# Order of the weighted expert sums in the last stage of a two-layer state-space and mixture-of-experts kernel

## What is computed

```
x = x + tanh(g_xattn[0]) * L0_xattn(ctx, layernorm(x))   # state-space scan, 16 states
x = x + tanh(g_ffn[0])   * L0_ffn(layernorm(x))          # 16 experts, 4 per token, and a shared one
x = x + tanh(g_xattn[1]) * L1_xattn(ctx, layernorm(x))   # a second scan
x = x + tanh(g_ffn[1])   * L1_ffn(layernorm(x))          # dense product, 8 low-rank experts, 2 per token
...
out, _ = jax.lax.scan(body, jnp.zeros_like(x), (gate_proj, up_proj, down_proj, cw.T))   # sum over experts of cw * y
```

## Time and profile before

| | us |
|---|---|
| median of 3 runs | 1586.72 |
| the runs | 1582.42, 1586.72, 1589.91 |
| profiled execution, own time | 1583.32 |
| its span | 1581.6 |
| DVE busy over the span | 1413.3 (89%) |
| TensorE busy, as modelled | 1255.5 (79%) |
| POOL busy | 794.9 (50%) |
| ScalarE busy | 836.6 (53%) |

### The profile page before, as it was taken

The page is one execution under the profiler, slowest core; times in us unless marked ns, Lnnn a source line. Parts: engine busy times, 40 slices in busy tenths (PEclk is TensorE's granted clock), DMA queues, the critical chain, the costliest instruction groups (busy, mean ns, idle before and its releaser), DMA issues.

```text
span 1581.6 us, 13941 instructions
## 1 busy us (share of the span) xinstructions
PE 1255.5 (79%) x4244; PEld 697.7 (44%) x4244; DVE 1413.3 (89%) x1462; ACT 836.6 (53%) x1341; POOL 794.9 (50%) x413
## 2 busy tenths in 40 slices
PE   6785677898689768977869998899988888806768
PEld 2321232443244224443526666566665666504444
DVE  4899989989999999998997999999899999967774
ACT  5754837473675455434855665556654444414332
POOL 0465446535553553360464556655556665575522
PEclk9898999799999998998989999999999999957889
DMA  7355546534553553350466778776877788564421
GB/s 249 99 135 128 106 115 143 139 97 134 139 139 82 145 132 99 92 160 28 95 179 212 226 243 293 236 237 232 267 260 244 269 269 270 204 194 127 130 81 54
DMA packets 99834, 264.27 MB, mean 167 GB/s; under 512 B 10832, under 2 KB 11344, under 8 KB 93616
## 3 DMA queue, kind: packets, MB, share of 16 engines
q1 hardware_dynamic: 87936, 225.36, 49.1%
q0 software_dynamic: 11440, 37.50, 7.2%
q10 hardware_dynamic: 384, 0.52, 0.1%
HBM read 233.73 MB, written 29.62 MB: 167 GB/s over the span
## 4 chain that ended last, share of the span: by engine, by line
DVE 37%; PE 30%; issue 8%; POOL 6%; DMA 6%; ACT 1%; DVEq 0%; SPq 0%; ACTq 0%; POOLq 0%
DVE state L1610 16%; DVE banks L1602 10%; PE banks L1108 9%; PE banks L1018 4%; PE banks L1119 4%; DMA expert_w<-in_moe_w 3%; DVE y_scan L1621 2%; PE banks L1075 2%; PE banks L1256 2%; DMA ys_d<-expert_out 1%; PE banks L1067 1%; PE banks L971 1%; POOL state L448 1%; POOL state L508 1%; PE banks L1087 1%
## 5 line engine op out<-in xcount | busy, mean ns | idle before, releaser
L448 POOL TENSOR_TENSOR state<-state,bc_rows 128x1024 f32<-128x1024 f32 x256 | 606.1, 2369 | 666.1 <-DVE banks L1602 665.9
L1018 PE MATMUL banks<-state,ident 128*128 128x512 f32 x640 | 336.6, 657 | 134.1 <-POOL state L448 133.9
L1610 DVE TENSOR_TENSOR_SCAN state<-decay,banks 128x1024 f32<-128x1024 f32 x176 | 402.1, 2285 | 18.0 <-PE banks L1018 13.5
L1602 DVE TENSOR_TENSOR banks<-du,bc_rows 128x1024 f32<-128x1024 f32 x256 | 315.3, 1232 | 13.2 <-issue 0.5
L1108 PE MATMUL banks<-z_gate,expert_w 128*128 128x256 f32 (+1 forms) x1504 | 285.7, 348 | 7.9 <-DMA expert_w<-in_moe_w 7.1
L673 ACT ACTIVATE decay<-delta,neg_a 128x511 f32<-128x511 f32 x352 | 231.4, 713 | 92.6 <-DVE state L1610 84.6
L1108 PEld LDWEIGHTS banks<-z_gate,expert_w 128*128 128x128 f32 x1504 | 250.3, 191 | 61.3 <-issue 21.0
L1018 PEld LDWEIGHTS banks<-state,ident 128*128 128x128 f32 x640 | 119.7, 202 | 324.7 <-POOL state L448 213.1
L1610 DVE TENSOR_TENSOR_SCAN state<-expert_w,banks 128x1024 f32<-128x1024 f32 x80 | 182.9, 2286 | 8.5 <-ACT expert_w L673 5.8
L1119 PE MATMUL banks<-expert_w,hidden 128*128 128x512 f32 x316 | 155.9, 609 | 2.9 <-DVE hidden L1631 2.9
L1621 DVE TENSOR_TENSOR y_scan<-y_scan,state 128x1024 f32<-128x1024 f32 x96 | 118.4, 1235 | 3.8 <-POOL state L448 3.8
(11 more groups left out here) (303 smaller groups left out, 1585.7 us busy)
## 6 DMA issues: line engine op xcount, KB each, us to landing
bc_rows<-bc_d SPq DMA_DIRECT2D x208, 512.0 KB, 5.0
expert_w<-in_moe_w SPq DMA_DIRECT2D x48, 1536.0 KB, 9.2
ys_d<-expert_out SPq DMA_DIRECT2D x32, 512.0 KB, 10.4
ctx_t<-in_ctxT SPq DMA_DIRECT2D x8, 512.0 KB, 6.8
x_res<-in_x SPq DMA_DIRECT2D x4, 1024.0 KB, 10.7
xn_d<-y_scan SPq DMA_DIRECT2D x4, 1024.0 KB, 7.7
ys_d<-expert_out SPq DMA_DIRECT2D x15, 256.0 KB, 9.4
out_x<-x_res SPq DMA_DIRECT2D x3, 1024.0 KB, 4.4
```

The lines of the kernel that those rows point to most:

```text
L448: nc.gpsimd.tensor_tensor(W[:, c % 4], W[:, c % 4], bcast2(BC[:, u, 1, :]), ALU.mult).then_inc(mulc_done, 1)
L1018: mm = nc.tensor.matmul(PS[:, m], ID[:, :], W[:, c % 4, m, :], start=False, stop=True, skip_group_check=True)
L1602: nc.vector.tensor_tensor(drive(s), DU[:, s % 2, 2 * h:2 * h + 2, :], bcast2(BC[:, u, 0, :]), ALU.mult).then_inc(mulb_done, 1)
L1610: nc.vector.tensor_tensor_scan(flat(W[:, c % 4]), flat(DAS[c % da_slots(s, i)]), flat(drive(s)), 0.0, ALU.mult, ALU.add).then_inc(scan_don ...
```

## The change

The sixteen sums of batches 1, 2 and 3 follow a list in which the fourth row block's sums stand as late as they can. `last` becomes the distance to the same block's sum before.

```diff
+            sums = ((0, 0), (0, 1), (0, 2), (1, 0), (1, 1), (0, 3), (2, 0), (1, 2),
+                    (2, 1), (1, 3), (2, 2), (3, 0), (2, 3), (3, 1), (3, 2), (3, 3))
+
             def combine(b, lo, hi):
                 for n in range(lo, hi):
-                    combine_one(b, n, n % QT, n // QT, QT)
+                    q, k = sums[n]
+                    combine_one(b, n, q, k, n - sums.index((q, k - 1)) if k else 0)
```

## The result

| | before | changed |
|---|---|---|
| median, us | 1587.97 (6 runs, 1582.42 to 1590.72) | 1571.55 (6 runs, 1566.96 to 1577.33) |
| ratio | 1 | 0.9898, 95% interval 0.9876 to 0.9921 |
| span of the profiled execution, us | 1581.6 | 1568.1 |

The change saves 16.4 us by the medians, 13.5 by the two spans. The spans also hold a difference that isn't the change's: the first sum of batch 0, where the tail begins, starts at 1399.94 before and at 1401.86 after. Over all fourteen profiles of this study it starts between 1399.2 and 1412.4, though nothing ahead of it was altered in any kernel. So I use the **tail length** from here on, from the start of that sum to the end of the last `lora_add`: 1575.42 + 3.26 - 1399.94 = 178.74 us before and 1561.92 + 3.26 - 1401.86 = 163.32 after, **15.4 us less**.

The account below looks back on a forecast made before the run. It took the tail to be a ring through L1410, TensorE and POOL, with L1410 held behind DVE's wait for the fourth block's gathers. -15.68 + 0.5 = -15.2 us, from 1585.6 to 1570.4 us; range 1563 to 1580.

Parts of the forecast that it names:

- Turn 0: First turn of the tail's loop: L1410 starts at 1437.54 instead of 1439.85, 2.31 us earlier.
- The extra 0.13: Turn 0, sums 0 and 1 in one block: the second waits for the first, 0.13 us charged in full.
- Turn 1: Second turn of the tail's loop: L1410 at 1469.47 instead of 1478.46, 8.99 us earlier, 6.68 of them new.
- Turn 2: Third turn of the tail's loop: L1410 at 1503.16 instead of 1518.84, 15.68 us earlier, 6.69 of them new.
- The fourth block's wait: DVE's wait for the fourth block's gathers, now behind seven sums in turns 1 and 2: nothing charged.
- I take 0: Store of a finished batch beside the fourth block's gathers: charged 0, bounds nothing or 2.5 us in full.
- slack of 1.4 us: Turns 1 and 2: the fourth block lands 1.4 us before DVE reaches its first sum.
- the covers: Time by which the gated product precedes TensorE's request: 1.7 us for turn 1's delay, 0.7 for turn 2's.
- DVE as the new end: Turn 2's DVE work through L1832 and gated product: done at 1525.0, TensorE asks at 1525.7, hidden by 0.7 us.
- TensorE's clock: L1410 to base in turns 1 and 2: mean 9.34 us used, +0.5 us in sum, bounds -1.4 and +2.9.
- The first: Rival: the wait returns at the fourth block's first sum, 3.0 us in turns 1 and 2; 1574.0 us, chance 0.15.
- the slower side: Rival: TensorE's lower clock adds 13.9 us per base stretch; with two, 12.6 us slower, 1598.2 us, chance 0.03.

Follow-up runs that it names:

- e8: The changed kernel run again with no edit; ratio 0.9931 to the kernel before, tail 164.17 us.
- e4: Changed kernel with the stores of batches 0 to 2 held until the next turn's mid_done; ratio 0.9918 to the kernel before, tail 164.60 us.
- e3: Kernel before, old list kept, with L1410 moved ahead of the third and fourth sum; ratio 0.9951 to the kernel before, tail 171.70 us.
- e10: Changed kernel with POOL's bias between block 2's second and third gathers and L1410 ahead of the third and fourth sum; ratio 0.9895, tail 163.59 us.
- e11: e10 with the stores also held until the next turn's mid_done; ratio 0.9879 to the kernel before, tail 159.32 us.
- e1: Changed kernel with only the four sums ahead of L1410 in the new order, the other twelve in the old; ratio 0.9928, tail 166.28 us.
- e5: Changed kernel, new list kept, with L1410 moved ahead of the third and fourth sum; ratio 0.9894 to the kernel before, tail 161.03 us.
- e12: The kernel of e11 run again; ratio 0.9883 to the kernel before, tail 159.86 us.

## Why the prediction was right

Forecast: 1570.4 us, 15.2 saved; measured 1571.55, with 15.4 saved in the tail. That the times differ by only 1.2 us is in part luck: the level from which I subtracted, 1585.6, was 2.4 under the median of the six runs, and the saving by the medians was 16.4. In e8 it was 11.7, below the 12.9 to 17 of the forecast, while the tails of both profiles lie inside it. By its steps, with places counted from the first sum of batch 0:

- **Turn 0**, forecast 2.31 earlier: L1410 at 39.91 before, 37.49 after, 2.42. The extra 0.13 for two sums in one block showed as 1.53 us for the pair against 1.41; three in one block took 2.32, again 0.12 to 0.13 for each dependence. The 0 that I read out of the Trainium skill for it (VectorE: DVE Perf Modes, section "The DRAIN you can't avoid") does not agree with these rows; the same section adds that a next operation that isn't held starts earlier, which the prediction left out and which the step of 0.66 us between sums of 0.75 agrees with. On the path little of it was left: the first sum behind the statistics started at 36.14 before and 36.19 after, since the two pairs of L1404 between took 2.92 us instead of 3.20.
- **Turn 1**, 8.99: 78.52 and 69.16, 9.36. POOL's first gather to the first sum took 21.45 (forecast 21.53), with L1822 held to the bias' end.
- **Turn 2**, 15.68: 118.90 and 103.00, 15.90. L1822 took 2.00 us instead of 0.17, held to the bias' end: POOL set the turn, and DVE had 1.8 us to spare.
- **The fourth block's wait, forecast 0: wrong**, 0.94 and 0.80 us. The step at fault is "I take 0" for the store: it was put inside a slack of 1.4 us that it exceeded. The landing came 31.10 us after POOL's first gather instead of 28.84, 2.26 later, near the upper bound of 2.5; less the 1.4 of slack, that is the 0.9. The Trainium skill's rule that queues share the engines (DMA: Bandwidth & Descriptors, section "Issuing engines are not separate DMA queues"), which I weighed at 0.6 us of wait, was nearer, and e4 showed the mechanism. The forecast of the time survived because the covers counted beside it held: e4 took the waits away and gained nothing.
- **DVE as the new end**, hidden by 0.7 us: L1390 ended at 1527.61, TensorE asked at 1528.86, 1.25 to spare.
- **TensorE's clock**, +0.5 in turns 1 and 2 with a mean of 9.34 for both: 9.68 and 9.83, 0.10 less and 1.42 more than before, +1.3 where +0.5 was put in. Turn 3, which the sum left at 10.52, took 9.58 and gave 0.94 back. So the sum over the turns was +0.2, by luck of terms and not by the account of them.
- **The rivals.** The first was right in kind and small in size. `base` stayed at 13.90 in all profiles of the changed kernel, so the slower side never came near.

## What to carry to other kernels

On an engine that works strictly in order, look for work that many wait on standing behind a wait that it doesn't share, and move the wait rather than the work: e3 moved the work and kept less than half of the gain. Place the awaited operand behind enough filler for both paths that leave the engine, then read which cover is left, since the next transfer (here a store) sits in it: it was free with the cover in place (e4) and cost about 3 us once that was spent (e10 against e11). And compare profiles over the stretch the edit can touch, less what the clock alone sets, when the whole program scatters by more than the edit is worth.

## What the runs showed of the hardware that I had not expected

- The last of four gathers, issued by POOL 0.36 us ahead of a store of 1 MB, took 5.9 us to land; with the store later it took 3.8.
- A sum (two inputs in SBUF) beside POOL's bias stood still for 4.5 us until the bias ended, while L1404 (one input in PSUM) ran beside it undisturbed. Of the operations with one input, in SBUF, the statistics (L1827, L1820) ran beside it at their usual 2.47 and 0.38 us, but L1822 was held to its end; no run here shows what sets them apart.
- The one gather issue of POOL that ran beside L1390 took 2.78 us instead of 0.95 and ended 0.8 us after it (1457.03 + 2.78 = 1459.81, L1390 until 1458.99; the same in turn 2, and before the change). POOL sets turns 1 and 2 of the changed kernel, so the lost 1.8 us count there, for at most the 0.85 and 1.83 us that L1822 was held; no run here took them away.
- TensorE's part of each turn, the same 48 instructions, took anything from 8.40 to 10.88 us, in no order with the length of the rest ahead of it: 3.88 us of rest in turn 1 was followed by 9.68, 2.1 us in turn 3 by 9.58, 10.4 us in turn 2 before the change by 8.41. In turn 3 before the change the granted clock was 1.00 through the 2.1 us of rest and fell only afterwards, to 0.50 (1.2 GHz) between 1551.7 and 1556.0, with the transposes and the first products under way; in turn 3 of e1, e3, e4, e5, e10 and e12 it stayed at 1.00.
